# A four-block transformer kernel on one core: split out-projections, a shorter RMS root, and a new order on every engine

## Time and profile before

| | us |
|---|---|
| Three executions | 2097.97, 2100.53, 2101.24 |
| The profiled execution | 2096.08 |
| Its span, first to last instruction | 2094.2 |
| PE busy | 1725.3 (82%) |
| DVE busy | 1591.4 (76%) |
| ACT busy | 1014.0 (48%) |
| POOL busy | 925.0 (44%) |
| Mean granted TensorE clock | 0.903 |

### The profile page before, as it was taken

How to read it: one execution, slowest core, us unless ns; L and a number is a source line. 1 busy time by engine, 2 the same in 40 slices (tenths; PEclk the granted TensorE clock), 3 DMA queues, 4 the chain that set the end, 5 groups by cost and what they waited for, 6 DMA issues and landing times.

```text
span 2094.2 us, 33718 instructions
## 1 busy us (share of the span) xinstructions
PE 1725.3 (82%) x12064; PEld 1120.0 (53%) x12141; DVE 1591.4 (76%) x3386; ACT 1014.0 (48%) x1997; POOL 925.0 (44%) x1166
## 2 busy tenths in 40 slices
...
GB/s 91 0 5 45 7 46 6 27 27 7 51 7 47 11 46 9 38 18 7 51 7 46 12 46 6 27 31 7 51 7 46 12 46 1 22 31 8 46 12 6
DMA packets 64617, 53.34 MB, mean 25 GB/s; under 512 B 6019, under 2 KB 63171, under 8 KB 64451
## 3 DMA queue, kind: packets, MB, share of 16 engines
...
## 4 chain that ended last, share of the span: by engine, by line
PE 45%; DVE 25%; SPq 9%; issue 7%; ACT 5%; POOL 5%; DMA 4%; DVEq 0%; ACTq 0%; POOLq 0%
PE bank L872 42%; SPq L299 8%; DVE rmax L743 7%; DMA kh<-part 4%; PE bank L868 3%; DVE prob L823 2%; DVE tree L653 2%; DVE stats L644 2%; ACT prob L464 2%; DVE rmax L740 1%; DVE inner L653 1%; SPq L311 1%; POOL rstd L343 1%; ACT xch L480 1%; DVE kk L666 1%
## 5 line engine op out<-in xcount | busy, mean ns | idle before, releaser
L743 DVE TENSOR_REDUCE rmax<-bank 128x1 f32<-128x512 f32 (+2 forms) x768 | 355.7, 504 | 131.3 <-PE bank L872 130.9
L464 ACT ACTIVATE prob<-bank 128x512 f32<-128x512 f32 x640 | 354.4, 598 | 136.1 <-PE bank L872 131.0
L872 PE MATMUL bank<-kh,qh 72*128 72x512 bf16 (+3 forms) x1024 | 289.2, 332 | 93.2 <-DMA kh<-part 52.8
L430 POOL TENSOR_TENSOR prob<-xdT,spread 128x512 f32<-128x512 f32 x128 | 167.5, 1309 | 377.4 <-ACT spread L464 377.4
L872 PE MATMUL bank<-wexpT,prob 128*128 128x128 f32 x2048 | 272.1, 279 | 5.3 <-issue 4.1
L872 PE MATMUL bank<-qh,kh 75*128 75x512 bf16 (+3 forms) x1024 | 256.6, 305 | 22.7 <-ACT prob L464 19.6
L872 PEld LDWEIGHTS bank<-wexpT,prob 128*128 128x128 f32 x2048 | 255.2, 193 | 18.5 <-issue 12.4
L872 PEld LDWEIGHTS bank<-kh,qh 72*128 72x128 bf16 x1024 | 108.5, 106 | 211.4 <-DVE rmax L743 71.8
L464 ACT ACTIVATE spread<-bank 128x512 f32<-128x512 f32 x128 | 76.5, 597 | 296.0 <-PE bank L872 209.5
L690 DVE RECIPROCAL wkb<-wkb 128x512 f32<-128x512 f32 x64 | 213.3, 3332 | 0.5 <-POOL wkb L376 0.5
L872 PE MATMUL bank<-maskb,identb 128*128 128x128 bf16 x1024 | 210.8, 237 | 0.0
...
## 6 DMA issues: line engine op xcount, KB each, us to landing
...
```

The costliest lines, as they stand in the source:

```text
L430: raised(pool.tensor_tensor(ug[:, e % 4, :], xdT[:, :], spread[e // 2 % 2][:, :], ALU.mult), "ug_side")
L464: raised(act.activation(dst, src, func, **kw), signal)
L743: last = dve.tensor_reduce(rmax[:, j, h:h + 1], S[n % 2][:, col:col + (j + 1) * P], AX_X, ALU.max)
L872: return pe.matmul(out_, w, x, start=start, stop=stop, **kw)
```

## The change

The matmuls of each out-projection are issued as four steps, one for each tile of tokens, with a signal each (`wo_ps` and `cmv_ps` count to four). RMS norm's root is taken directly: `rms_scale = (var * (1 + RMS_EPS) + RMS_EPS * LN_EPS) ** -0.5`, ahead of root4. ACT's norm3 waits for norm4 and norm_rms of the batch before, and norm4 stands in lag 3 at the start of the list rather than in lag 2 near its end. Every engine has a new order. Nine kinds of `busy` step are defined, two matmuls of constants each; no order names them.

```diff
 PER_BATCH = dict(
-    x_even=8, x_odd=8, stats=len(LNS), **{f"moments{n}": 1 for n in LNS}, **{f"root{n}": 3 for n in LNS}, **{f"shift{n}": 1 for n in LNS},
-    rms_step=5, rms_shift=1,
+    x_even=8, x_odd=8, stats=len(LNS), **{f"moments{n}": 1 for n in LNS}, **{f"root{n}": 2 if n == 4 else 3 for n in LNS}, **{f"shift{n}": 1 for n in LNS},
+    rms_step=3, rms_shift=1,
...
 ORDER = dict(
     sp="""
-        2:heads 0:load 2:max_rows 4:store
+        4:store 2:heads 0:load 2:max_rows
...
     pool="""
-        4:u5 4:u7 4:u9 0:root0 4:u11 1:r_sig0 4:u13 4:u15 1:gated0 1:wk0 1:r_sig1 1:wk1 4:root7 1:rwkv0 1:gated1 2:root4 2:root_rms 1:r_sig2 1:rwkv1 1:wk2
-        1:gated2 1:wk3 1:r_sig3 2:rope_sum0 2:rope_sum1 2:rest0 2:rest1 2:part_lo0 1:gated3 2:part_lo1 1:rwkv2 1:rwkv3 1:root2 3:root6 1:res 0:x1_gain
-        0:x1_bias 1:cmr_sig 1:cmr_sum 3:gate_rest 3:gate_lo 0:root1 3:u1 1:root3 3:u3
+        4:u3 1:wk0 4:u5 1:r_sig0 4:u7 4:u9 4:u11 1:gated0 0:root0 4:u13 1:r_sig1 4:u15 1:rwkv0 4:root7 1:r_sig2 1:wk1 1:wk2 1:gated1 2:root_rms 2:root4
+        1:rwkv1 1:gated2 1:r_sig3 1:wk3 2:rope_sum0 1:gated3 2:rope_sum1 2:rest0 2:rest1 1:rwkv2 2:part_lo0 1:rwkv3 2:part_lo1 1:res 1:root2 0:x1_gain
+        3:root6 0:x1_bias 0:root1 1:cmr_sig 1:cmr_sum 3:gate_rest 3:gate_lo 1:root3 3:u1
...
     act="""
-        2:cmr_tanh 4:gate_hi 4:gate_mid 4:gT_out 1:norm1 4:spread1 1:mix_before0 1:mix_before1 1:mix_before2 4:spread3 2:norm3 4:spread5 2:xbT_out 3:vaug
...
-        3:exp35 3:exp36 3:exp37 3:exp38 3:exp39 3:pvT_out1 2:norm4 3:attT_out 1:norm2 3:norm6 1:mix_before3 1:mix_before4 3:xdT_out 0:norm0 1:cmk_tanh0
-        3:route_exp 1:cmk_tanh1 1:cmk_tanh2 1:cmk_tanh3 2:values
+        2:cmr_tanh 1:norm1 3:norm4 4:gate_hi 4:gate_mid 4:gT_out 1:mix_before0 1:mix_before1 1:mix_before2 4:spread1 2:norm3 4:spread3 2:xbT_out 1:k_exp0
...
+        3:pvT_out0 3:exp35 3:exp36 3:exp37 2:part_mid1 3:exp38 3:exp39 3:pvT_out1 1:norm2 3:attT_out 0:norm0 1:mix_before3 1:mix_before4 3:norm6
+        1:cmk_tanh0 1:cmk_tanh1 3:xdT_out 1:cmk_tanh2 3:route_exp 1:cmk_tanh3 2:values
...
     dve="""
-        3:rowmax14 1:mix0 3:rowmax15 3:rowmax16 4:u4 3:rowmax17 1:mix1 3:rowmax18 3:rowmax19 1:mix2 3:rowmax20 0:moments0 3:rowmax21 1:clamp0 3:rowmax22
...
-        3:max_parts 1:wkv0 2:tree5 1:ksum0 2:tree6 1:clamp2 1:kv1 2:tree7 4:yd 1:ksum1 4:moments7 1:inverse0 1:kvsum1 1:kv2 1:wkv1 2:yb 2:moments4
-        1:inverse1 1:clamp3 1:kvsum2 1:wkv2 1:ksum2 1:ksum3 2:rope_mul0 2:rope_mul1 2:rope_mul2 1:kv3 2:rope_mul3 1:inverse2 1:kvsum3 1:wkv3 1:inverse3
-        3:attend0 3:attend1 1:x2 1:moments2 3:yc 3:moments6 2:rowmax0 1:mix3 1:mix4 2:rowmax1 2:rowmax2 3:route_logits 2:rowmax3 1:silu0 2:rowmax4 1:silu1
-        3:route_probs 2:rowmax5 3:largest0 1:silu2 2:rowmax6 3:others 1:silu3 3:largest1 3:gates 2:rowmax7 0:moments1 2:rowmax8 1:y0 2:rowmax9 2:rowmax10
-        3:u0 2:rowmax11 1:moments3 2:rowmax12 3:u2 2:rowmax13
+        4:u2 3:rowmax13 1:mix1 3:rowmax14 1:mix2 3:rowmax15 0:moments0 3:rowmax16 3:rowmax17 1:clamp0 4:u4 3:rowmax18 3:rowmax19 1:ksum0 3:rowmax20
+        3:rowmax21 4:u6 3:rowmax22 1:kv0 3:rowmax23 3:rowmax24 1:kvsum0 3:rowmax25 3:rowmax26 3:rowmax27 1:wkv0 3:rowmax28 4:u8 2:tree0 3:rowmax29
+        3:rowmax30 1:clamp1 3:rowmax31 3:rowmax32 4:u10 2:tree1 2:tree2 3:rowmax33 3:rowmax34 2:tree3 3:rowmax35 4:u12 3:rowmax36 3:rowmax37 3:rowmax38
+        4:u14 3:rowmax39 3:max_parts 1:inverse0 2:tree4 1:clamp2 1:kv1 2:tree5 2:tree6 2:tree7 1:ksum1 1:kvsum1 4:yd 4:moments7 1:wkv1 1:kv2 1:ksum2
+        1:clamp3 2:yb 2:moments4 1:inverse1 1:ksum3 1:kv3 1:kvsum2 1:wkv2 1:kvsum3 2:rope_mul0 2:rope_mul1 1:wkv3 2:rope_mul2 2:rope_mul3 1:inverse2
+        1:inverse3 3:attend0 1:x2 1:moments2 3:attend1 3:yc 3:moments6 1:mix3 1:mix4 0:moments1 1:silu0 1:silu1 2:rowmax0 2:rowmax1 3:route_logits
+        2:rowmax2 1:silu2 2:rowmax3 3:route_probs 2:rowmax4 1:silu3 3:largest0 2:rowmax5 3:others 2:rowmax6 3:largest1 3:gates 2:rowmax7 2:rowmax8 1:y0
+        2:rowmax9 2:rowmax10 1:moments3 3:u0 2:rowmax11 2:rowmax12 0:mix0
     """,
     pe="""
-        3:maxT 4:expert12 4:expert13 4:expert14 1:k2 4:expert15 3:score0 3:score1 1:r2 3:score2 3:score3 1:v2 3:score4 3:score5 2:leafT0 3:score6 3:score7
...
-        3:score32 2:attn_v 3:score33 3:score34 3:score35 3:score36 3:score37 3:back0 3:score38 3:score39 3:weigh12 3:weigh13 3:weigh14 3:weigh15
-        1:read_out 3:back1 3:attT 3:attn_out 1:xn2T 2:row0 3:xdT 2:row1 2:row2 3:centroids 1:cmk0 2:row3 2:row4 1:cmk1 1:cmk2 2:row5 2:row6 1:cmk3 2:row7
-        3:shared 1:cmr 2:row8 1:cmv 2:row9 3:gT 2:row10 3:gb0 2:row11 2:row12 3:gb1 0:xnT 3:biases 2:row13 3:gb2 2:row14 3:expert0 3:gb3 2:row15 2:row16
...
+        4:expert13 4:expert14 4:expert15 1:r2 3:score0 3:score1 1:v2 3:score2 3:score3 1:k3 3:score4 3:score5 2:leafT0 3:score6 3:score7 2:leafT1 3:score8
...
+        3:score36 3:back0 3:score37 3:score38 3:score39 1:read_out0 1:read_out1 1:read_out2 1:read_out3 3:weigh12 3:weigh13 3:weigh14 3:weigh15 2:attn_v
+        3:back1 3:attT 1:xn2T 3:attn_out 1:cmk0 1:cmk1 3:xdT 2:row0 2:row1 3:centroids 1:cmk2 2:row2 2:row3 1:cmk3 2:row4 2:row5 1:cmr 2:row6 1:cmv0
+        1:cmv1 1:cmv2 1:cmv3 2:row7 2:row8 3:shared 2:row9 2:row10 3:gT 0:xnT 2:row11 2:row12 3:gb0 3:biases 3:gb1 3:expert0 3:gb2 2:row13 2:row14 3:gb3
+        3:expert1 1:xbT 2:row15 2:row16 3:gb4 0:k0 2:row17 3:expert2 0:v0 2:row18 2:row19 0:r0 3:gb5 3:expert3 2:row20 2:row21 3:gb6 3:expert4 2:row22
...
+        3:expert11 3:gb15 0:k2 2:maxT 3:expert12
...
                 until(pool, b, f"moments{n}")
                 raised(pool.tensor_tensor(var[:, n, :], mv[:, n, :, 1], eps_ln[:, :], ALU.add), f"root{n}")
-                raised(pool.tensor_tensor(minus[:, n, :], mv[:, n, :, 0], minus_one[:, :], ALU.mult), f"root{n}")
+                if n != 4:
+                    raised(pool.tensor_tensor(minus[:, n, :], mv[:, n, :, 0], minus_one[:, :], ALU.mult), f"root{n}")
                 until(pool, b, f"root{n}", 1)
                 raised(pool.tensor_tensor(rstd[:, n, :], var[:, n, :], exponent[:, :], ALU.pow), f"root{n}")
                 until(pool, b, f"root{n}")
+                if n == 4:
+                    until(pool, b, "rms_step", 2)
                 raised(pool.tensor_tensor(shift[:, n, :], minus[:, n, :], rstd[:, n, :], ALU.mult), f"shift{n}")
 
             def root_rms(b):
 
-                until(pool, b, "root4")
-                raised(pool.tensor_tensor(rms_a[:, :], mv[:, 4, :, 1], rstd[:, 4, :], ALU.mult), "rms_step")
+                until(pool, b, "moments4")
+                raised(pool.tensor_scalar(rms_a[:, :], mv[:, 4, :, 1], 1.0 + RMS_EPS, RMS_EPS * LN_EPS, ALU.mult, ALU.add), "rms_step")
+                raised(pool.tensor_tensor(minus[:, 4, :], mv[:, 4, :, 0], minus_one[:, :], ALU.mult), "rms_step")
                 until(pool, b, "rms_step", 1)
-                raised(pool.tensor_tensor(rms_b[:, :], rms_a[:, :], rstd[:, 4, :], ALU.mult), "rms_step")
-                until(pool, b, "rms_step", 2)
-                raised(pool.tensor_tensor(rms_a[:, :], rms_b[:, :], eps_rms[:, :], ALU.add), "rms_step")
+                raised(pool.tensor_tensor(rms_scale[:, :], rms_a[:, :], exponent[:, :], ALU.pow), "rms_step")
                 until(pool, b, "rms_step", 3)
-                raised(pool.tensor_tensor(rms_root[:, :], rms_a[:, :], exponent[:, :], ALU.pow), "rms_step")
-                until(pool, b, "rms_step", 4)
-                raised(pool.tensor_tensor(rms_scale[:, :], rms_root[:, :], rstd[:, 4, :], ALU.mult), "rms_step")
-                until(pool, b, "rms_step", 5)
                 raised(pool.tensor_tensor(rms_shift[:, :], minus[:, 4, :], rms_scale[:, :], ALU.mult), "rms_shift")
...
-                "norm2": lambda b: norm(b, 2, hat, x2, "post_hat"), "norm3": lambda b: norm(b, 3, xb, y0, "xb"),
+                "norm2": lambda b: norm(b, 2, hat, x2, "post_hat"), "norm3": lambda b: (until(act, b - 1, "xc"), until(act, b - 1, "xch"), norm(b, 3, xb, y0, "xb")),
...
-            def by_tokens(bk, t, w, signal):
-
-                for j in range(J):
-                    for c in range(C):
-                        last = mm(bk[:, j * P:(j + 1) * P], t[:, c, j * P:(j + 1) * P], w[:, c, :], c == 0, c == C - 1)
-                raised(last, signal)
-
-            def read_out(b):
-                until(pe, b, "rwkv")
-                until(pe, b, "kv")
-                by_tokens(T1, inner, wo, "wo_ps")
+            def by_tokens(bk, t, w, j):
+
+                for c in range(C):
+                    last = mm(bk[:, j * P:(j + 1) * P], t[:, c, j * P:(j + 1) * P], w[:, c, :], c == 0, c == C - 1)
+                return last
+
+            def read_out(b, j):
+                if j == 0:
+                    until(pe, b, "rwkv")
+                    until(pe, b, "kv")
+                raised(by_tokens(T1, inner, wo, j), "wo_ps")
+
+            def keep_busy(bk):
+
+                for _ in range(2):
```

(21 more changed lines are left out.)

56 lines of the change are left out of this document (43 added, 13 removed).

## The result

The changed kernel takes 1982.86 us (median of 4 runs, 1979.55 to 1986.61), the kernel before 2099.25 us in the same series (4 runs, 2097.38 to 2101.24).

A forecast was written before the change was run, and what follows sets the result against it. No engine was full; the bound was a 118.1 us turn of row stretch, score stretch and copy gap. Terms -3.3 - 1.5 + 0.6 = -4.2 us over 13 turns, and -2 at the ends, gave 2044 us; 8-in-10 range 2014 to 2084.

The forecast's parts named there:

- that term: Start of the rows: rowmax0 follows row0's start by 1.3 us instead of 0.75, costing +0.6 us per turn.
- The row stretch, -3.3: First row product to end of max_parts: DVE work falls 2.5 us, idle 0.8 to 0.9, together -3.3 us per turn.
- the other bound: Row stretch: if only 1 us of DVE's idle time stays, the stretch falls by 6.7 us.
- the first rival: Gap and row stretch: PE stays at 2.4 GHz through the gap, -6 us per turn, 2020 us; chance 0.12.
- its unrounded sum, -7.6: Whole turn at full PE clock: -6.7 - 1.5 + 0.6 us, before 1.6 was left to mutual waits.
- The score stretch, -1.5: From max_parts to the last score: DVE loses 2.0 us and gains 0.4, -1.5 us per turn.
- fourth rival: Score stretch: four more DVE scans or products slow beside POOL, +4.3 us per turn, about 2100 us; chance 0.06.
- Xch and the root, 0.78: Score stretch: the shorter root brings xch 2 to 3 us sooner, saving PE's 0.78 us wait for xcT.
- The ends, -2: Fill, two short turns and drain: little DVE work to lose, -2 us in all.
- At nothing: Split out-projections, unused keep_busy steps, the store's move and norm4's move: no effect; norm4 would cost 1.65 us if uncovered.
- The second: Scores gain nothing as inverse0 delays r2, row idle time stays: -1.9 us per turn, 2073 us; chance 0.20.
- The third: Gap: late rwkv3 holds read_out, the chain outlasts the copies; 6 us delay gives +1.8 per turn, 2124 us; chance 0.12.

The follow-up runs named there:

- experiment 1: Kernel before with 24 constant matmuls added on PE in the gap's two pauses, ahead of the first row product; 2062.49 us, ratio 0.9847.
- experiment 3: Changed kernel with the gap's moved work back behind row0 and rowmax0, plus 24 constant matmuls behind attn_out; 2048.49 us, ratio 0.9756.
- experiment 11: Changed kernel with ten constant matmuls added between attn_out and cmk0, in PE's last pause of the gap; 1971.44 us, ratio 0.9387.
- experiment 5: Changed kernel with the whole score stretch in the old order on all four engines, except attn_v, root_rms, rwkv2 and rwkv3; 2064.84 us, ratio 0.9822.
- experiment 9: Changed kernel with seven extra POOL products per turn, each reading two SBUF tiles, behind rwkv0; 2020.81 us, ratio 0.9623.
- experiment 10: Changed kernel with thirteen extra POOL memsets per turn, which read nothing, behind rwkv0; 1980.82 us, ratio 0.9421.
- experiment 12: Kernel before with only the new RMS root, root_rms ahead of root4; 2083.5 us, ratio 0.9918.
- experiment 6: Changed kernel with the old ten-instruction RMS root, root4 first; 1983.6 us, ratio 0.944.
- experiment 7: Changed kernel with each out-projection as one step and one signal again; 1982.23 us, ratio 0.9441.
- experiment 8: Changed kernel with SP's old order, the store behind max_rows; 1984.04 us, ratio 0.9445.
- experiment 4: Changed kernel with only the start of the score stretch as before (inverse0 late, r2 behind score1), PE's k3 staying early; 2158.69 us, ratio 1.0275.
- Experiment 2: Changed kernel with the gap's moved work put back behind row0 and rowmax0, no added matmuls; 2077.91 us, ratio 0.9891.

## Why the prediction was right and wrong

**The frame held.** The turn as unit, the gap that stays (17.4 forecast, 17.9 measured, ended by the copies), the work that moves into it, and that the row stretch gives more than the score stretch were right. The same holds for DVE's busy time in the row stretch (49.5 forecast, 50.2 measured) and PE's in the gap (13.4 and 13.8). Rowmax0 follows row0 by 0.48 us and not by 1.3; that term was 0.8 too high, and the gap 0.5 longer, which cancels. The sum missed in two terms and at the ends.

**The row stretch, -3.3.** The step that failed is "if all of that stays ... I take 0.8 to 0.9 us of idle gone", chosen "because PE is nearly as full". Measured, between rowmax0 and the end of max_parts the same turns lost 6.1 us: 1.8 by DVE's work (51.55 to 49.77 busy) and 4.3 by its idle time, near the other bound that the prediction had written down (-6.7). (Its 5.1 us of idle time took the busy time of a longer window; on its own stretch, 57.18 us with 51.55 busy, it is 5.6, and the bound -7.1.) The idle time was not PE being full, it was PE being slow: experiment 1 takes 4.7 us out of the stretch, 3.0 in the mean turn, with the clock alone and no DVE work moved. In the mean turn the stretch and the gap together lost 4.6 us, for 2.7 forecast. This is the first rival, given 0.12, with its sign "a granted clock of 1.00 through the whole row stretch" to the letter. That its unrounded sum, -7.6, is what the mean turn lost is luck: it had 6.1 of it in rows and gap and 1.5 in the scores, where 4.6 and 3.0 were measured. The argument against it was that pauses of 2 to 3 us remain in the gap. They do, one of 2.74 us, and the clock falls there to 0.77; but it is at 1.00 again when the rows start, where before it stood at 0.50 until 1022, 7 us into them:

```profile
1014.00:1018.00 4.00, 3.33 (x16) 2.55 (x17) 2.58 (x5) 1.84 (x6) 0.00 (x0) 0.50 0.00 2
1018.00:1022.00 4.00, 4.00 (x15) 2.49 (x16) 1.77 (x6) 1.15 (x4) 2.53 (x2) 0.50 0.00 0
```

(windows of 4 us of before, columns as in the earlier trace rows.) The Trainium skill (TensorE: Matmul & The Clock Gate, What's actually happening) was cited in the prediction for exactly this, with a sum near -6 beside it; experiments 1 and 3 and the gap of experiment 11 agree with it, and the chance should have followed.

**The score stretch, -1.5.** The step that failed is "DVE loses the same 2.0 us and gains 0.4": a count of instructions at unchanged durations. Measured -3.0 per mean turn, DVE's busy time -4.8 in the windows. The prediction had the price in its hand, the same scan at 1.22 and 2.29 us, and used it only for a loss, as fourth rival. The old order already paid for collisions, 137.6 us of busy time, and the new one pays 71.9: the groups of before and after show who, experiment 5 puts 40 us of it back by order alone, and experiments 9 and 10 show that POOL's reads do this and its writes don't. That POOL was busier in the score stretch than elsewhere said that such collisions were there to be lost or avoided; the direction could not be read off the busy shares, only from which POOL instruction stands beside which tree step in each list.

**Xch and the root, 0.78 inside that term.** In the old order the root gave a gain (17 us, experiment 12), of which an unknown part is the wait, in the new one nothing (experiment 6), where ACT comes to norm_rms later than the root. The two gains don't add, though the sum assumed it.

**The ends, -2.** The sum had thirteen turns; these lost 7.7 us each between the profiled executions, 100.0. What it called fill, short turns and drain gave 14.8 and not 2: 6.0 ahead of the turns, 5.6 in the last interval, 3.2 behind it. In the fill the granted clock rose from 0.78 to 0.83; what shortened the drain, where no DVE instruction collides in either trace, was not followed.

**At nothing.** The split of the projections and the store are worth nothing that can be measured, as forecast (experiments 7 and 8); the busy steps stand in no order. Norm4's place was not tried alone.

**The other rivals.** The second (nothing gained in scores and idle) is refuted by the stretches; what it feared of inverse0 is the reverse of what experiment 4 shows. The third exists in experiment 5, where rwkv3 is late, and costs 3.9 us per turn there; but row0 is only 1.5 us later, far from the 4.2 to 6 us of its price, and the slower clock in the rows adds the rest. The fourth is the right mechanism with the wrong sign.

**What stays open.** How the 7.6 us per turn divide between clock, moved work and collisions can't be given as a sum: undoing the gap costs 6.8 and undoing the score stretch 5.6, which is more than there is, because each half needs the other. Experiment 2 warns against reading the 65 us as time won: it keeps nearly all of them (DVE 1529.6 us busy) and is only 24 us faster than the kernel before. By DVE group the largest parts of the 65 are ksum's scans (29.6) and the tree's 128x128 steps (28.5), less 19.4 that its 128x32 steps lose; no single pair of a POOL and a DVE instruction was tried.
